# Cross-attention in a decoder layer: twelve stretches of tiles a unit instead of sixteen, whole projections, and the side work of ScalarE, VectorE, GpSimd and the DMA queue at other slots

## The chip, the core and the metric

One core of a Trainium2 chip. The metric is device microseconds of one execution. TensorE (PE) multiplies into eight PSUM banks of 128x512 floats; VectorE (DVE), ScalarE (ACT) and GpSimd (POOL) work beside it; SyncE (SP) issues the DMAs of the stage told of here, all into one queue. Each engine runs its own instructions strictly in order, and engines wait for each other with semaphores.

## What is computed

A post-norm decoder layer on x of 16 batches of 256 rows of 512: self-attention with low-rank corrections, cross-attention over the channel axis, and a gated feed-forward with fp8 rounding, each followed by an addition and a layer norm. The change is in the cross-attention, where x and c are 256x512 per batch (256 channels, 512 positions), with 16 heads of 16 channels:

```python
q = jnp.einsum('oc,bct->bot', Wq, x) + bq[None, :, None]
k = jnp.einsum('oc,bct->bot', Wk, c) + bk[None, :, None]
v = jnp.einsum('oc,bct->bot', Wv, c) + bv[None, :, None]
scores = jnp.einsum('bhkt,bhks->bhts', q, k) * SCALE
p = jax.nn.softmax(scores, axis=-1)
out = jnp.einsum('bhts,bhks->bhkt', p, v)
x = _layernorm(x + Wo @ out + bo)
```

## The kernel before, in words

The program is a list of slots. Each engine has a generator for each phase (self-attention, cross-attention, feed-forward), and a list of turns interleaves the phases: the start of the cross-attention lies beside the end of the self-attention, the end beside the start of the feed-forward, and some 900 of its 1162 slots stand alone.

**Units and tiles.** A unit is half of a batch (8 heads), so there are U = 32 units, and a new one begins every S = 32 slots. An E tile is a 128x512 tile of scores for the exponential, an M tile the same product with the sides swapped, from which the row maximum is taken beforehand. In the steady stage a slot issues one E tile of one unit (L1271) and one M tile of a later unit (L1279); they use opposite halves of the PE rows. ScalarE turns an E tile into probabilities (L1136) and VectorE reduces an M tile to negated maxima (L1314). E tiles rotate over three banks, and so do M tiles: an M tile waits until the reduce of the tile three before it has freed its bank. M tiles of unit u stand in slots 32u+40 to 32u+71, its E tiles from 32u+82.

**Side work of PE.** Each unit has eight groups of values matmuls (L1236, four heads a group, from the probabilities into bank 7) and four projections (q, k, v, and the output projection o; functions `project_part` and `split3`, L85 to L87), all into bank 2. Each projection comes in two parts four slots apart, so 8 + 8 pieces of side work divide a unit's 32 slots into 16 stretches of two slots. A full projection leaves its bank one slot after its last part (`ends_in.get(slot - 1)`), by ScalarE for q, k and v, by VectorE for o, where an addition, BN_STATS and BN_AGGR stand together (L1335 to L1341).

**Stacks.** The float32 scores are made of three products of high and low parts. ScalarE copies the projection out, GpSimd splits it (L1057, L1059), and SP copies it into one of three stacks, six DMAs of 128 KB for q (slot 32u+20) and six for k (32u+25), at L959. The stack of unit u is that of unit u-3, so the q stack waits until the last E tile of u-3 is done (`s_e`), and the first M tile of u waits for all twelve DMAs. In every other unit SP loads the next c (512 KB, L916) between the two.

**Normalising.** Half a unit's output is in bank 7 with its sums. ScalarE copies it to `oc` at slots OUT_AT and OUT_AT + 16 (L1146); SP moves the sums to `xa_sums` one slot on (8 KB, L998); VectorE takes the reciprocal eight slots on (L1345); SP writes them to DRAM (`inv`, 8 KB, L1003) and reads them back, broadcast, into `xa_den` (256 KB, L1011); GpSimd multiplies and adds the halves (L1067, L1072); ScalarE and GpSimd split the sum for the output projection (L1175, L1077). All of these stand in their engines' queues at slots counted from OUT_AT = 101.

Of the kernel before, what the change touches and what calls it, by code (L numbers as in the profile page):

```python
# [15 lines left out]
P = 128  # L16
# [746 lines left out]
XPROBS = 12  # L763
# [3 lines left out]
def cross_attention_phase(nc, ctx, mem, banks, shared, left, a, x1_dram, x2_dram, inv_dram, ones_dram, wg_dram,  # L767
# [30 lines left out]
    prob = values.sb("xa_prob", [P, XPROBS, D], F32)  # L798
# [3 lines left out]
    ol = mem("output").sb("xa_ol", [P, 2, groups, D], F32R)  # L802
# [17 lines left out]
    MAX_AT, TURN_AT, EXP_AT = S + 8, 2 * S + 10, 2 * S + 18  # L820
    BATCH = 2 * S
    OUT_AT = EXP_AT + 19
# [3 lines left out]
    part_slots = {}  # L826
    for u in range(U):
        part_slots["q", u] = [S * u + 2, S * u + 6]
        part_slots["k", u] = [S * u + 10, S * u + 14]
    for b in range(NB):  # L830
        part_slots["v", b, 0] = [BATCH * b + 26, BATCH * b + 30]
        part_slots["v", b, 1] = [BATCH * b + 50, BATCH * b + 54]
        part_slots["o", b, 0] = [BATCH * (b + 2) + 58, BATCH * (b + 2) + 62]
        part_slots["o", b, 1] = [BATCH * (b + 3) + 18, BATCH * (b + 3) + 22]
    for t in range(CC):
        part_slots["o", NB - 1, t] = [BATCH * (NB + 1) + n for n in ((26, 58), (60, 62))[t]]
    slot_of = {j: slots[-1] for j, slots in part_slots.items()}
    at = {j: n for n, j in enumerate(sorted(slot_of, key=lambda j: slot_of[j]))}
    parts_in, ends_in = {}, {}
    for job in part_slots:  # L840
        ends_in.setdefault(slot_of[job], []).append(job)
        for i, slot in enumerate(part_slots[job]):
            parts_in.setdefault(slot, []).append((job, i))
# [7 lines left out]
    def in_turn(count, two, three, begin):  # L851
        at_bank = [two[n % 2] if n < begin else three[n % 3] for n in range(count)]
        before = [max((m for m in range(max(0, n - 4), n) if at_bank[m] == at_bank[n]), default=None)
                  for n in range(count)]
        return at_bank, before

    mb, mb_before = in_turn(len(m_order), (3, 4), (3, 4, 1), (S + 1) * 4)
    eb, eb_before = in_turn(S * U, (5, 6), (5, 6, 0), S * 2)
    SLOTS = range(max(slot_of.values()) + 12)
# [80 lines left out]
    def sync(sp):  # L940
# [38 lines left out]
        for slot in SLOTS:  # L979
# [19 lines left out]
            if (un := output_half(slot, 9)):  # L999
# [5 lines left out]
            if (un := output_half(slot, 14)):  # L1005
# [14 lines left out]
            for job in ends_in.get(slot - 9, []):  # L1020
# [17 lines left out]
    def gpsimd(pool):  # L1038
# [9 lines left out]
        for slot in SLOTS:  # L1048
            yield
            for job in ends_in.get(slot - 2, []):  # L1050
                if job[0] in "qk":
# [28 lines left out]
            if (b := batch(slot, -17)):  # L1080
                low_x(pool, wait, b)
# [713 lines left out]
```

## Times and profile before

| | us |
|---|---|
| median of 3 runs | 2126.02 (2120.32 to 2133.86) |
| the profiled execution, its own time | 2100.74 |
| its span | 2098.9 |
| busy in the span: PE / DVE / ACT / POOL | 1948.0 / 1513.9 / 1133.2 / 997.0 |
| of the 600 us from 1000 to 1600, cross-attention alone: PE / DVE / ACT / POOL | 590.44 / 485.41 / 477.26 / 266.69 |
| one reduce of an M tile (L1314), mean | 0.681 |
| granted PE clock there | 0.99 of full speed |
| share of the 16 DMA engines busy there, and GB/s | 0.63, 112 |

PE is busy for nearly the whole of the steady stage, but a busy PE is not one at its peak: of matmuls that run at once each is counted, and a matmul's end is modelled. All DMAs in the stage are issued by SP.

### The profile page before, as it was taken

The page shows a single profiled execution, that of the slowest core. Times are in us where ns is not written, and L with a number is a line of the kernel's source. Part 1 is how long each engine was busy: PE and PEld are TensorE (multiplying, and loading weights), DVE is VectorE, ACT ScalarE, POOL GpSimd, SP SyncE. Part 2 cuts the span into 40 slices and gives each one's busy share as a digit, 9 for nine tenths or more (in the row PEclk, how much of TensorE's full clock was granted, in tenths as well). Part 3 has the DMA queues.
Part 4 walks back from the last instruction along what each step waited for, and adds up shares of the span by engine and source line. Part 5 has one row for each costly group of instructions (what it writes and reads, how often), then busy time and mean ns, then how long its engine had stood idle before and what let it go on. Part 6 is the DMA issues. An engine that isn't in the chain of part 4 may idle for free.

```text
span 2098.9 us, 31715 instructions
## 1 busy us (share of the span) xinstructions
PE 1948.0 (93%) x11390; PEld 1045.0 (50%) x11424; DVE 1513.9 (72%) x2635; ACT 1133.2 (54%) x2117; POOL 997.0 (47%) x980
## 2 busy tenths in 40 slices
PE   3799999899999888999999999999999898999997
PEld 1667777677767643344434444444444333444443
DVE  4246585566656656777878888887888728999997
ACT  3144444344434433677878877887888673333331
POOL 6345455455554531444444444443444326666664
PEclk9899999999999877999999999999999989999999
DMA  4678786777778653556776655556665510111111
GB/s 138 114 132 138 157 144 130 144 135 161 148 124 150 117 98 52 87 89 127 133 123 112 109 106 107 107 108 103 113 101 105 152 53 11 51 41 41 41 61 41
DMA packets 149515, 220.55 MB, mean 105 GB/s; under 512 B 41463, under 2 KB 50167, under 8 KB 148615
## 3 DMA queue, kind: packets, MB, share of 16 engines
q1 hardware_dynamic: 139886, 217.74, 53.7%
q10 hardware_dynamic: 9472, 0.79, 0.4%
q8 instruction: 90, 1.47, 0.4%
q14 instruction: 67, 0.55, 0.1%
HBM read 83.95 MB, written 32.02 MB: 55 GB/s over the span
## 4 chain that ended last, share of the span: by engine, by line
PE 52%; DMA 19%; DVE 12%; POOL 6%; ACT 3%; issue 3%; SPq 3%; ACTq 0%; POOLq 0%; DVEq 0%
PE bank L1565 7%; PE bank L1236 7%; PE bank L1271 7%; PE bank L85 6%; DMA xa_sums<-xa_oc 5%; PE bank L1541 4%; PE bank L86 4%; PE bank L87 4%; PE bank L1279 4%; DMA sa_kst<-sa_part_kl 4%; DMA inv<-xa_sums 4%; PE bank L506 3%; DMA xa_den<-inv 2%; PE bank L531 2%; DVE sa_mneg L574 2%
## 5 line engine op out<-in xcount | busy, mean ns | idle before, releaser
L1314 DVE TENSOR_REDUCE xa_mneg<-bank 128x1 f32<-128x512 f32 x1024 | 657.8, 681 | 193.7 <-PE bank L1279 190.1
L1136 ACT ACTIVATE xa_prob<-bank 128x512 f32<-128x512 f32 x1024 | 568.9, 600 | 204.9 <-PE bank L1271 195.7
L1279 PE MATMUL bank<-xa_kst,xa_qst 48*128 48x512 f32 x1024 | 411.3, 475 | 23.1 <-DVE xa_mneg L1314 14.9
L1271 PE MATMUL bank<-xa_qst,xa_kst 49*128 49x512 f32 x1024 | 398.4, 460 | 14.3 <-ACT xa_prob L1136 13.9
L402 ACT ACTIVATE sa_prob<-bank 128x512 f32<-128x512 f32 x256 | 152.4, 598 | 370.3 <-PE bank L531 369.7
L1271 PEld LDWEIGHTS bank<-xa_qst,xa_kst 49*128 49x128 f32 x1024 | 161.7, 189 | 329.5 <-ACT xa_prob L1136 257.6
L1236 PE MATMUL bank<-xa_prob,xa_v 128*32 128x512 f32 x2048 | 283.8, 627 | 0.0
L1473 POOL TENSOR_TENSOR ff_total<-ff_prod,ff_mag 128x512 f32<-128x512 bf16 x128 | 194.5, 1520 | 108.6 <-DVE ff_mag L1589 108.6
L574 DVE TENSOR_REDUCE sa_mneg<-bank 128x2 f32<-128x512 f32 x256 | 164.2, 682 | 51.6 <-PE bank L543 51.3
L1279 PEld LDWEIGHTS bank<-xa_kst,xa_qst 48*128 48x128 f32 x1024 | 164.0, 190 | 58.5 <-DVE xa_mneg L1314 38.4
L1517 ACT ACTIVATE ff_gelu<-bank 128x512 bf16<-128x512 f32 x128 | 75.5, 592 | 160.9 <-PE bank L1565 158.7
L1057 POOL CAST xa_part_q<-xa_raw_q 128x512 fp32r<-128x512 f32 x32 | 19.5, 610 | 269.7 <-ACT xa_raw_q L1154 248.0
L531 PE MATMUL bank<-sa_qst,sa_kst 97*128 97x256 f32 x512 | 113.8, 306 | 15.0 <-DMA sa_qst<-sa_mrow 15.0
L531 PEld LDWEIGHTS bank<-sa_qst,sa_kst 97*128 97x128 f32 x512 | 93.5, 196 | 60.1 <-issue 28.6
L1541 PE MATMUL bank<-ff_wo,ff_hq 128*128 128x512 bf16 x504 | 117.2, 385 | 5.3 <-DVE ff_hq L1596 4.6
L1565 PE MATMUL bank<-ff_xq,ff_wg 128*128 128x512 bf16 x498 | 116.5, 383 | 3.4 <-ACT ff_gelu L1517 1.8
L1565 PE MATMUL bank<-ff_xq,wg 128*128 128x512 bf16 x500 | 114.2, 382 | 2.0 <-ACT ff_gelu L1517 1.0
L543 PE MATMUL bank<-sa_kst,sa_qst 96*128 96x256 f32 x512 | 93.9, 301 | 16.6 <-DVE sa_mneg L574 7.9
L1582 DVE TENSOR_TENSOR ff_prod<-bank,ff_gelu 128x512 bf16<-128x512 f32 x128 | 87.1, 680 | 22.6 <-PE bank L1565 18.6
L588 DVE TENSOR_TENSOR sa_xnat<-bank,sa_xnat 128x512 f32<-128x512 f32 x128 | 87.2, 681 | 19.9 <-PE bank L87 18.4
L344 POOL CAST sa_part_qh<-sa_raw 128x512 fp32r<-128x512 f32 x32 | 19.5, 610 | 155.3 <-DMA sa_kst<-sa_part_kl 129.3
L543 PEld LDWEIGHTS bank<-sa_kst,sa_qst 96*128 96x128 f32 x512 | 76.2, 201 | 24.5 <-DVE sa_mneg L574 16.4
(185 smaller groups left out, 3730.6 us busy)
## 6 DMA issues: line engine op xcount, KB each, us to landing
xa_qst<-xa_part_q SPq DMA_DIRECT2D x192, 128.0 KB, 5.4
xa_kst<-xa_part_k SPq DMA_DIRECT2D x192, 128.0 KB, 6.8
sa_qst<-sa_part_qh SPq DMA_DIRECT2D x64, 256.0 KB, 6.2
sa_kst<-sa_part_kh SPq DMA_DIRECT2D x64, 256.0 KB, 9.0
xa_den<-inv SPq DMA_DIRECT2D x64, 256.0 KB
sa_xraw<-xT SPq DMA_DIRECT2D x8, 1024.0 KB, 8.5
sa_qst<-sa_part_ql SPq DMA_DIRECT2D x32, 256.0 KB, 6.0
sa_kst<-sa_part_kl SPq DMA_DIRECT2D x32, 256.0 KB, 10.3
```

The source lines that it names most:

```text
L402: act.activation(prob[:, e % PROBS, :, :], eb[e % 2][:, :], ACT.Exp, scale=S_SCALE)\
L531: last = pe.matmul(eb[e % 2][:, t * L:(t + 1) * L], k[0:97, j, b * L + t * P:b * L + (t + 1) * P], q[0:97, j, b * L:(b + 1) * L], start=Tr ...
L543: last = pe.matmul(mb[m % 2][:, t * L:(t + 1) * L], q[0:96, j, b * L + t * P:b * L + (t + 1) * P], k[0:96, j, b * L:(b + 1) * L], start=Tr ...
L574: dve.tensor_reduce(mneg[:, u % 2, 4 * j + 2 * b:4 * j + 2 * b + 2], mb[m % 2][:, :].rearrange("p (t n) -> p t n", t=2), AX.X, ALU.max, ne ...
L1136: act.activation(prob[:, e % XPROBS, :], banks[eb[e]][:, :], ACT.Exp, scale=X_SCALE)\
L1236: last = pe.matmul(ob[32 * j:32 * j + 32, :], v[(u // 2) % 2][:, t, half, 4 * (u % 2) + j, :], prob[:, (S * u + 4 * quad + j) % XPROBS, :] ...
L1271: pe.matmul(banks[eb[e]][:, :], kst[u % 3][rows_of, head // 2, t * P:(t + 1) * P], qst[u % 3][rows_of, head // 2, :], start=True, stop=Tru ...
L1279: pe.matmul(banks[mb[m]][:, :], qst[u % 3][rows_of, n // 8, t * P:(t + 1) * P], kst[u % 3][rows_of, n // 8, :], start=True, stop=True).the ...
L1314: dve.tensor_reduce(mneg[:, u % 2, column:column + 1], banks[mb[m]][:, :], AX.X, ALU.max, negate=True).then_inc(s_mfree, 1)
L1473: pool.tensor_tensor(total[:, n % 4, :], prod[:, n % 4, :], mag[:, n % 4, :], ALU.add).then_inc(s_hs, 1)
L1541: last = pe.matmul(lb[n % 2][:, :], hq[p % 2][:, h, t * P:(t + 1) * P], wo[:, h, :], start=(h == 0), stop=(h == HT - 1))
L1565: last = pe.matmul(banks[n % 2][:, :], wg[q][:, k, c, h % 4 * P:(h % 4 + 1) * P], xq[p % 2][:, c, :], start=(c == 0), stop=(c == DC - 1))
```

## The change

Projections are issued whole, in one slot, at 2 (q), 10 (k), 18 (o) and 26 (v) of every 32, and values groups in slots of their own that alternate three and five slots apart. So 12 pieces of side work divide a unit, with two or three slots of tiles between them. E tiles start two slots later, the work counted from OUT_AT moves five slots and is drawn closer together, ScalarE, VectorE and GpSimd leave the projection bank three to six slots after the projection, and there are 16 probability tiles, each its own tensor, instead of 12. Buffers of the feed-forward move to make room for four of them; its work is the same. The start of its turns follows the last E tile.

```diff
-XPROBS = 12
+XPROBS = 12, 16
...
-    MAX_AT, TURN_AT, EXP_AT = S + 8, 2 * S + 10, 2 * S + 18
+    MAX_AT, TURN_AT, EXP_AT = S + 8, 2 * S + 10, 2 * S + 20
     BATCH = 2 * S
-    OUT_AT = EXP_AT + 19
+    GROUP = 4
+    VALUES_AT = (EXP_AT + 9, EXP_AT + 12)
+    OUT_AT = EXP_AT + 22
...
-        part_slots["q", u] = [S * u + 2, S * u + 6]
-        part_slots["k", u] = [S * u + 10, S * u + 14]
+    LEAVES = {"q": 3, "k": 6, "v": 3, "o": 3}
+        slot_of["q", u] = S * u + 2
+        slot_of["k", u] = S * u + 10
...
+            slot_of["v", b, t] = BATCH * b + S * t + 26
+            slot_of["o", b, t] = BATCH * (b + 2) + S * t + 50
...
-            if (un := output_half(slot, 9)):
+            if (un := output_half(slot, 7)):
...
-            if (un := output_half(slot, 14)):
+            if (un := output_half(slot, 11)):
...
-            if (un := output_half(slot, 21)):
+            if (un := output_half(slot, 16)):
...
-            if (un := unit(slot, OUT_AT + 41, 1)):
+            if (un := unit(slot, OUT_AT + 35, 1)):
...
-            if (un := unit(slot, EXP_AT + 34, 1)):
-                values(un[0], 7)
-            if (un := unit(slot, EXP_AT + 6, S - 7)) and un[1] % 4 == 0:
-                values(un[0], un[1] // 4)
+            for odd in range(2):
+                if (un := unit(slot, VALUES_AT[odd])) and un[1] % (2 * GROUP) == 0:
+                    values(un[0], un[1] // GROUP + odd)
...
-            for job, i in parts_in.get(slot, []):
-                project_part(job, i)
+            for job in jobs_in.get(slot, []):
+                for i in range(2):
+                    project_part(job, i)
...
-            for job in ends_in.get(slot - 1, []):
+            for job in jobs_in.get(slot - LEAVES["o"], []):
...
-            if (un := output_half(slot, 8)):
+            if (un := output_half(slot, 6)):
                 k = 2 * un[0] + un[1]
                 wait.wait_ge(s_sums, 16 * (k + 1))
                 dve.reciprocal(sums[:, :], sums[:, :]).then_inc(s_inv, 1)
```

Unchanged are the slots of the stacks (STACK_AT = 20 and 25), of the M tiles (MAX_AT), and of the loads of c and x.

SP's queue in one unit of the steady stage, one in which c is loaded too. `xa_qst` and `xa_kst` are the stacks, `xa_sums` and `inv` the sums and their reciprocals, `xa_oc` 134 or 145 is the first half and 135 or 146 the second. Before:

```order
L959 DMA xa_qst_129<-xa_part_q 16x4x512 [waits xa_e,xa_pl]
L959 DMA xa_qst_129<-xa_part_q 16x4x512 x5
L998 DMA xa_sums<-xa_oc_135 128x1x16 [waits xa_oc1]
L916 DMA xa_craw<-c 128x2x512 [waits xa_xlow,xa_xhi]
L959 DMA xa_kst_128<-xa_part_k 16x4x512 [waits xa_pl]
L959 DMA xa_kst_128<-xa_part_k 16x4x512 x5
L1003 DMA inv<-xa_sums 4x32x16 [waits xa_den1,xa_inv]
```

Now:

```order
L965 DMA xa_qst_129<-xa_part_q 16x4x512 [waits xa_e,xa_pl]
L965 DMA xa_qst_129<-xa_part_q 16x4x512 x5
L1017 DMA xa_den_147<-inv 128x1x512 [waits xa_o,xa_back]
L922 DMA xa_craw<-c 128x2x512 [waits xa_xlow,xa_xhi]
L965 DMA xa_kst_128<-xa_part_k 16x4x512 [waits xa_pl]
L965 DMA xa_kst_128<-xa_part_k 16x4x512 x5
L1004 DMA xa_sums<-xa_oc_146 128x1x16 [waits xa_oc1]
L1030 DMA x<-xa_x_0_117 128x512 [waits xa_y]
L1009 DMA inv<-xa_sums 4x32x16 [waits xa_den1,xa_inv]
```

The sums of the second half stood between the two stacks and now stand behind the k stack; the first half's `xa_den` stood ahead of the q stack and now stands behind it.

VectorE's queue over the same slots: TENSOR_REDUCE frees an M tile's bank, `xa_mrow` is the turned row of maxima, SCALAR_TENSOR_TENSOR to BN_AGGR take an output projection out of its bank. Before:

```order
L1345 RECIPROCAL xa_sums<-xa_sums 128x16 [waits xa_sums]
L1314 TENSOR_REDUCE xa_mneg<-bank 128x1 [waits xa_mb] x2
L1335 SCALAR_TENSOR_TENSOR xa_x_1_118<-bank,xa_bo,xa_x_1_118 128x512 [waits xa_pj]
L1338 BN_STATS xa_stats<-xa_x_1_118 128x6 [waits xa_pjfree]
L1341 BN_AGGR xa_mv<-xa_stats 128x2 [waits xa_nm,xa_bn]
L1314 TENSOR_REDUCE xa_mneg<-bank 128x1 [waits xa_mb] x11
L1327 CAST xa_mrow<-bank 32x128 [waits xa_row0,xa_mb]
L1314 TENSOR_REDUCE xa_mneg<-bank 128x1 [waits xa_mb] x3
L1345 RECIPROCAL xa_sums<-xa_sums 128x16 [waits xa_sums]
```

Now:

```order
L1348 SCALAR_TENSOR_TENSOR xa_x_1_118<-bank,xa_bo,xa_x_1_118 128x512 [waits xa_pj]
L1351 BN_STATS xa_stats<-xa_x_1_118 128x6 [waits xa_pjfree]
L1354 BN_AGGR xa_mv<-xa_stats 128x2 [waits xa_nm,xa_bn]
L1327 TENSOR_REDUCE xa_mneg<-bank 128x1 [waits xa_mb] x11
L1358 RECIPROCAL xa_sums<-xa_sums 128x16 [waits xa_sums]
L1327 TENSOR_REDUCE xa_mneg<-bank 128x1 [waits xa_mb] x10
L1340 CAST xa_mrow<-bank 32x128 [waits xa_row0,xa_mb]
L1327 TENSOR_REDUCE xa_mneg<-bank 128x1 [waits xa_mb] x6
L1358 RECIPROCAL xa_sums<-xa_sums 128x16 [waits xa_sums]
```

The reciprocal of the second half stood behind the reduce of slot 29 of 32 and now stands behind that of slot 0, with the reduces of slots 1 to 10 behind it; that of the first half moved from slot 13 to 16.

## Rows read from the trace of the kernel before

**Rows 1.** The rows of L1290 from 1000 to 1600 us, one each unit.
```profile
L1290 PE MATMUL bank<-ident,xa_mneg x21: 283/284/397, 1019.3 to 1573.7; 128*32 128x128 f32 x21
```

**Rows 2.** Timeline of PE: start, us, engine, line, operation, names, count, [idle before].
```profile
1011.18 1.07 PE L1236 MATMUL bank<-xa_prob,xa_v 128*32 128x512 f32 x8
1012.18 0.50 PE L1271 MATMUL bank<-xa_qst,xa_kst 49*128 49x512 f32 x1
...
1012.85 0.50 PE L85 MATMUL bank<-xa_xh,xa_wqh 128*128 128x512 f32 x1
1013.18 0.40 PE L86 MATMUL bank<-xa_xh,xa_wql 128*128 128x512 f32 x1
1013.42 0.39 PE L87 MATMUL bank<-xa_xl,xa_wqh 128*128 128x512 f32 x1
1013.74 0.49 PE L1271 MATMUL bank<-xa_qst,xa_kst 49*128 49x512 f32 x1
```

**Rows 3.** Timeline of SP's queue, two units; us is the issuing, not the transfer.
```profile
1277.51 3.85 SPq L959 DMA_DIRECT2D xa_qst<-xa_part_q  x6
...
1282.58 3.77 SPq L959 DMA_DIRECT2D xa_kst<-xa_part_k  x6
1288.45 0.55 SPq L1003 DMA_DIRECT2D inv<-xa_sums  x1
...
1296.06 0.65 SPq L1011 DMA_DIRECT2D xa_den<-inv  x1
...
1302.04 0.58 SPq L1003 DMA_DIRECT2D inv<-xa_sums  x1
1304.02 0.64 SPq L1011 DMA_DIRECT2D xa_den<-inv  x1
1304.76 4.11 SPq L959 DMA_DIRECT2D xa_qst<-xa_part_q  x6
...
1309.90 3.78 SPq L959 DMA_DIRECT2D xa_kst<-xa_part_k  x6
1316.47 0.55 SPq L1003 DMA_DIRECT2D inv<-xa_sums  x1
1319.49 0.65 SPq L1011 DMA_DIRECT2D xa_den<-inv  x1
```

**Rows 4.** The same of two more units, the slowest of each kind.
```profile
1053.77 3.85 SPq L959 DMA_DIRECT2D xa_qst<-xa_part_q  x6
...
1074.70 0.65 SPq L1011 DMA_DIRECT2D xa_den<-inv  x1
...
1194.13 4.29 SPq L959 DMA_DIRECT2D xa_qst<-xa_part_q  x6
...
1211.27 0.65 SPq L1011 DMA_DIRECT2D xa_den<-inv  x1
```

**Rows 5.** Timeline of PE at a unit's last E tile.
```profile
1303.81 0.49 PE L1271 MATMUL bank<-xa_qst,xa_kst 49*128 49x512 f32 x1
```

**Rows 6.** Timeline of VectorE around a reciprocal and an output projection.
```profile
1316.19 0.25 DVE L1345 RECIPROCAL xa_sums<-xa_sums 128x16 f32<-128x16 f32 x1 [0.67 <-DMA xa_sums<-xa_oc]
...
1317.50 0.74 DVE L1335 SCALAR_TENSOR_TENSOR xa_x<-bank,xa_bo,xa_x 128x512 f32<-128x512 f32 x1
...
1319.10 2.45 DVE L1314 TENSOR_REDUCE xa_mneg<-bank 128x1 f32<-128x512 f32 x4
```

**Rows 7.** Busy time by stretch: PE, PEld, DVE, ACT, POOL, PE clock, DMA, GB/s.
```profile
1071.00:1075.00 4.00, 1.37 (x10) 0.51 (x8) 1.17 (x2) 2.37 (x5) 0.37 (x1) 1.00 0.41 86
1075.00:1078.50 3.50, 3.50 (x15) 1.17 (x15) 1.52 (x3) 0.87 (x2) 1.51 (x2) 0.51 0.51 140
...
1660.00:1673.00 13.00, 8.09 (x29) 3.12 (x26) 5.03 (x9) 4.24 (x9) 3.80 (x3) 0.61 0.14 49
```

**Rows 8.** The chain that ended last, 1200 to 1300 us: start, us, what.
```profile
1241.22 3.80 DMA xa_den<-inv
...
1246.45 1.29 POOL xa_of L1072
```

More of the change, by code:

```diff
@@ L797, in cross_attention_phase @@
     oh = r.sb("xa_oh", [P, 2, groups, D], F32R)
-    prob = values.sb("xa_prob", [P, XPROBS, D], F32)
+    prob = [values.sb(f"xa_prob{n}", [P, D], F32) for n in range(XPROBS[0])]
     oc = [rounding.sb(f"xa_oc{n}", [P, D], F32) for n in range(2)]
@@ L801, in cross_attention_phase @@
     of = parts.sb("xa_of", [P, D], F32)
-    ol = mem("output").sb("xa_ol", [P, 2, groups, D], F32R)
+    output = mem("output")
+    ol = output.sb("xa_ol", [P, 2, groups, D], F32R)
+    prob += [output.sb(f"xa_prob{n}", [P, D], F32) for n in range(*XPROBS)]
     r = mem("cross_small")
@@ L848, in cross_attention_phase, with in_turn @@
     m_at = {job: n for n, (_, _, job) in enumerate(sorted(m_order, key=lambda m: m[:2]))}
-    def in_turn(count, two, three, begin):
-        at_bank = [two[n % 2] if n < begin else three[n % 3] for n in range(count)]
-        before = [max((m for m in range(max(0, n - 4), n) if at_bank[m] == at_bank[n]), default=None)
+    def in_turn(count, few, more, begin):
+        places = [few[n % len(few)] if n < begin else more[n % len(more)] for n in range(count)]
+        before = [max((m for m in range(max(0, n - 2 * len(more)), n) if places[m] == places[n]), default=None)
                   for n in range(count)]
-        return at_bank, before
+        return places, before
     mb, mb_before = in_turn(len(m_order), (3, 4), (3, 4, 1), (S + 1) * 4)
     eb, eb_before = in_turn(S * U, (5, 6), (5, 6, 0), S * 2)
+    place, prob_before = in_turn(
+        S * U, range(XPROBS[0]), [*range(*XPROBS), *range(XPROBS[0])], S * 2)
     SLOTS = range(max(slot_of.values()) + 12)
@@ L1068, in gpsimd @@
                     .then_inc(s_o, 1)
-            if (un := unit(slot, OUT_AT + 39, 1)):
+            if (un := unit(slot, OUT_AT + 34, 1)):
                 u = un[0]
@@ L1133, in scalar @@
                 wait.wait_ge(s_e, e + 1)
-                wait.wait_ge(s_av, (e - XPROBS) // 4 + 1)
-                left.values(wait)
-                act.activation(prob[:, e % XPROBS, :], banks[eb[e]][:, :], ACT.Exp, scale=X_SCALE)\
+                if prob_before[e] is not None:
+                    wait.wait_ge(s_av, prob_before[e] // GROUP + 1)
+                elif place[e] < XPROBS[0]:
+                    left.values(wait)
+                else:
+                    left.output(wait)
+                act.activation(prob[place[e]][:, :], banks[eb[e]][:, :], ACT.Exp, scale=X_SCALE)\
                    .then_inc(s_exp, 1)
@@ L1225, in mb_free, with values @@
                 wait.wait_ge(s_mfree, mb_before[m] + 1)
-        def values(u, quad):
-            half, t = quad // 4, quad % 4
-            wait.wait_ge(s_exp, S * u + 4 * quad + 4)
+        def values(u, group):
+            half, t = group // 4, group % 4
+            wait.wait_ge(s_exp, S * u + GROUP * (group + 1))
             wait.wait_ge(s_pjfree, at["v", u // 2, 1] + 1)
@@ L1742, in build @@
         start += size
-    stretches["output_rest"] = stretches["output"][0] + 8192, 12288
+    stretches["output_rest"] = stretches["output"][0] + 16384, 4096
+    stretches["sums_rest"] = stretches["sums"][0] + 8192, 4096
     def mem(name):
```

64 lines of the change are left out of this document (30 added, 34 removed).

## The prediction, made before the changed kernel was run

> **What bounds the kernel now.** I read the busy time of the steady stage first, then the timeline of PE to price each piece of its program, then the period of a unit, and then SP's queue and the chain, to see what fills the difference. The transpose of L1290 comes once a unit: 20 units in 554.4 us, 27.7 us each [rows 1]. PE's own work is less. From the starts: two slots of tiles 0.67, a group of values 1.00, half a projection 0.89 [rows 2]. A unit has 32 slots, 8 groups and 8 halves: 10.7 + 8.0 + 7.1 = 25.8 us. So 1.9 us of each unit are waits, though PE looks busy. The engines that follow have room (VectorE 485 and ScalarE 477 of 600 us), so the waits are for particular things.
>
> The one that matters is the queue of DMAs. The q stack is issued 0.95 us after the start of the E tile that frees its buffer [rows 5, 3]. Then twelve stack DMAs, the sums, and every other unit c go out. When all of it has landed is seen by a small transfer issued behind it: `inv` is 8 KB, and SP issues `xa_den` as soon as it lands. With nothing ahead that takes 1.98 us (1302.04 to 1304.02); behind a k stack and c 7.6 (1288.45 to 1296.06), behind a k stack alone 3.0 [rows 3]. The small transfer lands with the big ones ahead of it. From the issue of the q stack to that landing it is 18.55 us in the unit with c and 14.7 in the one without [rows 3]; the slowest of each are 20.9 and 17.1 [rows 4]. I take 18.55 and, between 14.7 and 17.1, 15.8.
>
> The Trainium skill (DMA: Bandwidth & Descriptors, Queues, rings and completion order) says that completion in general is not first in, first out per issuing engine, since a DMA spread over few of the 16 engines owes nothing to the others. By that a small transfer might land early; here the rows show it does not.
>
> **The change, part by part.** I count slots modulo 32, with 36 for slot 4 of the next unit.
>
> *PE's own time.* The second half of a whole projection costs three more matmuls, L86 and L87 start 0.24 apart: 0.72 instead of 0.89 [rows 2]. A projection is 1.61 and a unit 10.7 + 8.0 + 6.4 = 25.2 us, 0.7 less. Fewer stretches of tiles save nothing more: a slot of tiles costs 0.335 wherever it stands.
>
> *The output projection on VectorE.* It holds the queue for 1.60 us (1317.50 to 1319.10), and reduces follow 0.6 apart [rows 6]. It now stands behind the reduce of slot 21. Tile 21 issued at 0, that reduce starts at about 1.1, the projection is left at 1.7, the reduces of 22 and 23 start at 3.3 and 3.9 and free their banks about 0.7 later, at 4.0 and 4.6. PE (values at 21 and 24) wants M tiles 25 and 26 at 3.35 and 3.7. It loses 0.9 us, about what such waits cost before.
>
> *ScalarE, probabilities.* Its copies now stand where PE does a values group or a projection; 16 tiles give the later groups room. I price this at nothing: the cover is its 20% of idle time. Without it each would cost its own 0.6 us.
>
> *Sums of the second half.* This is the term that decides. SP had them between the stacks; now they are behind the k stack in order, so they are issued only when those twelve DMAs are out, and land with them. VectorE's reciprocal waits for them behind the reduce of slot 32, and the reduces of 33 to 42 are behind the reciprocal. With three banks, M tiles 33 to 35 still go; M tile 36 needs the reduce of 33. Already before, the reciprocal waited 0.67 us for its sums [rows 6], there behind only the q stack.
> Count from E tile 19, the last of its unit. Sums land at 0.95 + 15.8 = 16.75 us (with c 0.95 + 18.55 = 19.5). The next reduce follows 0.2 after the reciprocal, which is 0.25 long, starts, and the bank is free 0.7 later (a reduce is 681 ns in the mean): M tile 36 starts at 17.65 (20.4). PE comes to it by 17 slots, 4 groups and 2 projections: 5.7 + 4.0 + 3.2 + 0.9 = 13.8. So it stands 3.8 us (6.6).
> From M tile 36 to the next E tile 19 are 15 slots, 4 groups, 2 projections and 0.3 for reduces in a row: 5.0 + 4.0 + 3.2 + 0.3 = 12.5. The period is 30.15 us without c and 32.9 with it.
> This holds wherever a k stack stands just ahead of second-half sums: stacks of units 3 to 31, 29 of them, 13 with c. Mean (16 x 30.15 + 13 x 32.9) / 29 = 31.4, against 27.7: **+3.7 x 29 = +107 us**.
>
> *The clock.* When PE waited 2.6 us for a k stack in 1071 to 1075, the granted clock was 0.51, the lower level of 1.2 GHz, in the following 3.5 us [rows 7]. Half of 3.5 us is lost: 1.7. After each of 29 longer waits: **+49 us**. Bounds: nothing, and 5.1 us a time (148), as in 1660 to 1673, where PE had two waits close together and the mean clock was 0.61, 13 x 0.39 [rows 7]; I take the row with one wait.
> The Trainium skill (TensorE: Matmul & The Clock Gate, HAM oscillation) describes a loop that waits for a DMA at each step and starts every step at the low clock. The trace agrees as far as its one long wait goes. By that rule the lower bound of nothing is unlikely.
>
> *The first M tile.* It waits for the k stack (slot 40). Stacks start two slots later, with the E tiles, but now PE is already late by more, so this adds nothing to the above. If the sums did not stall, it would be next (below).
>
> *The rest of the chain.* After the sums come `inv` (1.98), `xa_den` (3.8), a multiply and an addition, 1.3 each: 8.5 us [rows 3, 8]. The copy of the result at slot 45 comes 6.9 + 0.5 us after M tile 36, itself 0.9 after the sums: 8.3. It is just in time, and adds 0 to 0.3 us a unit. The first half's sums have nothing large ahead of them. The head, the three last units and the feed-forward: two to five slots each, below 5 us, 0.
>
> **Sum.** 2100.7 + 107 + 49 = 2257 us in the profiled execution's own time. The median of the runs shown is 25.3 us above that execution, so 2282 in their terms.
>
> **The rivals.**
> 1. *The sums stall, the clock stays up*: +107, 2233. For it: with 1.9 us of waits in each unit the stage's clock was 0.99. Against: those are in several pieces, and the one piece of 2.6 us did bring it down.
> 2. *The sums do not stall* (they land early, as the skill's sentence allows, or VectorE has them in time). Then the k stack sets the time at M tile 40: 0.95 + 18.4, then 11 slots, 3 groups and 2 projections, 9.9: 29.25 with c, and 0.95 + 15.6 + 9.9 = 26.45 without (18.4 and 15.6 are the landings above less 0.2 for the small transfer); mean 27.7, as before: 2126, no change. It decides if a small transfer behind six big ones takes below 3 us; rows 3 speak against it.
> 3. *Faster*: neither stall; the stage runs at PE's 25.2 + 0.9 = 26.1 us, -1.6 x 29 = -46: 2080. It needs the stacks with c to land within about 16 us of their issue, against 18.55.
> 4. *Worse*: the clock falls for longer after the waits of 6.6 us and the copy at slot 45 comes late too: 2282 + 96 = 2378.
>
> **Chances.** Forecast with the clock loss 0.58, rival 1 0.20, rival 4 0.06: slower 0.84. Rival 2 0.09, rival 3 0.07. Some of rival 2's place lies beyond 1% to either side, but evenly. A difference of 1%, 21 us, is about what can be told from no change. The range reaches from rival 1 with the shortest landings of rows 3 (14.7 for 15.8, 16 x 1.1 = 18 us less, and as much again on the units with c: 2195) to the forecast with the clock loss at 4 us a time (2350); it leaves the forecast's neighbours 2 and 3 out.
>
> **What would show it.** Right: the reciprocal behind slot 32 waits 4 to 8 us for `xa_sums`; M tile 36 has the largest idle time of PE, released by VectorE; the period of L1302, the transpose, is near 30 and 33 us in turn plus the clock's part; PE's granted clock falls once a unit; landing of `xa_sums` has two clusters, about 2 us and 6 to 9. Wrong: periods near 27 with waits at M tile 40 for `xa_kst` (rival 2), or a period of 26 (rival 3). What would make it wrong is a sums transfer that overtakes the k stack, or k stacks that start earlier than the last E tile allows.

## The result, and the profile after

The changed kernel takes 2332.7 us (median of 4 runs, 2323.5 to 2339.8), the kernel before, run beside it, 2123.2 (2102.9 to 2133.9): a ratio of 1.100 with a 95% interval of 1.091 to 1.109. It is slower by 10%. The profiled execution's own time is 2323.5 us with a span of 2321.7, so 223 us more than the 2100.7 of before, where the prediction has 156.

The steady stage shows the whole of it. Its row of busy time, from 1000 to 1600 us (columns: stretch, us, busy PE, PEld, DVE, ACT, POOL, then PE clock, share of the DMA engines, GB/s):

```profile
1000.00:1600.00 600.00, 480.15 (x2659) 216.63 (x2659) 365.97 (x636) 359.44 (x686) 210.17 (x217) 0.88 0.54 87
```

Every engine has a fifth to a quarter less work in it than before, the DMA engines too (112 GB/s before), and the granted clock fell from 0.99 to 0.88. No engine became the bound; waits did. The transpose that comes once a unit is L1302 now:

```profile
L1302 PE MATMUL bank<-ident,xa_mneg x17: 283/284/286, 1016.6 to 1589.2; 128*32 128x128 f32 x17
```

That is 572.6 us for 16 units, 35.8 each, against 27.7 [rows 1]. The 8.1 us more, over the 29 units that the prediction counts, would be 235, so the stage holds the whole loss. Waits of the same stretch (who, for whom: us in all, times, the longest):

```profile
DVE xa_sums L1358 <- DMA xa_sums<-xa_oc: 143.1, 17, 10.0
PEld bank L1292 <- DVE xa_mneg L1327: 135.5, 49, 8.7
POOL xa_of L1075 <- DMA xa_den<-inv: 123.5, 17, 8.5
PE bank L1292 <- DVE xa_mneg L1327: 118.2, 33, 8.3
```

One wait a unit, 8.4 us in the mean, for the second half's sums; and PE's wait for the reduce queued behind it. From the page of the whole execution, the line of the chain that ended last (shares of the span), and the group of the reciprocal (count | busy, mean ns | idle before it, and for what):

```profile
PE 41%; DMA 20%; SPq 11%; DVE 11%; ACT 7%; POOL 5%; issue 3%; ACTq 0%; POOLq 0%; DVEq 0%
...
L1358 DVE RECIPROCAL xa_sums<-xa_sums 128x16 f32<-128x16 f32 x64 | 15.9, 248 | 253.7 <-DMA xa_sums<-xa_oc 253.7
```

One unit with c, followed through three timelines (start, us, engine, line, what, [idle before]). SP's queue:

```profile
1311.18 3.81 SPq L965 DMA_DIRECT2D xa_qst<-xa_part_q  x6
1315.10 0.66 SPq L1017 DMA_DIRECT2D xa_den<-inv  x1
1315.86 0.40 SPq L922 DMA_DIRECT2D xa_craw<-c  x1
1316.31 5.16 SPq L965 DMA_DIRECT2D xa_kst<-xa_part_k  x6
1321.52 0.59 SPq L1004 DMA_DIRECT2D xa_sums<-xa_oc  x1
```

VectorE:

```profile
1319.73 2.58 DVE L1327 TENSOR_REDUCE xa_mneg<-bank 128x1 f32<-128x512 f32 x4
1331.00 0.25 DVE L1358 RECIPROCAL xa_sums<-xa_sums 128x16 f32<-128x16 f32 x1 [8.69 <-DMA xa_sums<-xa_oc]
1331.17 3.01 DVE L1327 TENSOR_REDUCE xa_mneg<-bank 128x1 f32<-128x512 f32 x5
```

PE, where the matmul that waits is M tile 36:

```profile
1319.86 0.50 PE L1284 MATMUL bank<-xa_qst,xa_kst 49*128 49x512 f32 x1
...
1320.90 1.06 PE L1249 MATMUL bank<-xa_prob,xa_v 128*32 128x512 f32 x8
...
1324.15 0.50 PE L1292 MATMUL bank<-xa_kst,xa_qst 48*128 48x512 f32 x1
1324.49 0.39 PE L1284 MATMUL bank<-xa_qst,xa_kst 49*128 49x512 f32 x1
1331.85 1.39 PE L1292 MATMUL bank<-xa_kst,xa_qst 48*128 48x512 f32 x2 [6.98 <-DVE xa_mneg L1327]
1332.45 0.62 PE L1284 MATMUL bank<-xa_qst,xa_kst 49*128 49x512 f32 x1
1333.17 1.94 PE L1249 MATMUL bank<-xa_prob,xa_v 128*32 128x512 f32 x8
```

The sums are issued at 1321.52, as soon as SP is through with the k stack, and are there at 1331.0, 19.8 us after the q stack's issue. The reduces, 0.6 apart till 1322.3, stop. PE has three banks, uses them, and stands for 7 us. Then it goes on at about half speed: the values group of L1249 takes 1.94 us where the one before the wait took 1.06. The granted clock by stretch, columns as above:

```profile
1312.00:1323.00 11.00, 10.74 (x72) 5.14 (x65) 9.34 (x16) 8.72 (x19) 1.35 (x5) 1.00 1.00 149
1323.00:1333.00 10.00, 3.02 (x12) 1.74 (x10) 2.00 (x5) 1.60 (x4) 1.14 (x1) 0.78 0.67 102
1333.00:1340.00 7.00, 7.00 (x32) 2.31 (x31) 3.87 (x7) 3.58 (x7) 4.43 (x4) 0.58 0.34 112
```

### The profile page after: what moved, and what is told of

Same layout as the page of the kernel before. It is cut to its first block, busy times and chain, and to the rows that moved or that the text cites. A ratio compares the mean times of both kernels' runs of the same rounds, so it can differ in the third digit from the quotient of the medians.

```text
span 2321.7 us, 31753 instructions
## 1 busy us (share of the span) xinstructions
PE 1982.9 (85%) x11424; PEld 1090.1 (47%) x11424; DVE 1497.9 (65%) x2635; ACT 1118.1 (48%) x2117; POOL 1000.8 (43%) x980
## 4 chain that ended last, share of the span: by engine, by line
PE 41%; DMA 20%; SPq 11%; DVE 11%; ACT 7%; POOL 5%; issue 3%; ACTq 0%; POOLq 0%; DVEq 0%
DMA xa_sums<-xa_oc 13%; SPq L965 9%; PE bank L1578 6%; PE bank L1249 5%; PE bank L1284 5%; PE bank L85 5%; ACT xa_prob L1148 4%; DMA sa_kst<-sa_part_kl 4%; PE bank L87 4%; PE bank L86 4%; PE bank L1554 4%; PE bank L1292 3%; PE bank L506 3%; PE bank L531 2%; DVE xa_mneg L1327 1%
## 5 line engine op out<-in xcount | busy, mean ns | idle before, releaser
L1327 DVE TENSOR_REDUCE xa_mneg<-bank 128x1 f32<-128x512 f32 x1024 | 642.6, 682 | 218.9 <-PE bank L1292 217.8
L1148 ACT ACTIVATE xa_prob<-bank 128x512 f32<-128x512 f32 x1024 | 550.5, 608 | 403.8 <-PE bank L1284 400.1
L1292 PE MATMUL bank<-xa_kst,xa_qst 48*128 48x512 f32 x1024 | 426.7, 508 | 201.9 <-DVE xa_mneg L1327 199.4
L1284 PE MATMUL bank<-xa_qst,xa_kst 49*128 49x512 f32 x1024 | 389.8, 470 | 16.2 <-ACT xa_prob L1148 16.1
L1284 PEld LDWEIGHTS bank<-xa_qst,xa_kst 49*128 49x128 f32 x1024 | 181.0, 203 | 328.7 <-ACT xa_prob L1148 221.8
L1249 PE MATMUL bank<-xa_prob,xa_v 128*32 128x512 f32 x2048 | 312.4, 686 | 0.0
L1292 PEld LDWEIGHTS bank<-xa_kst,xa_qst 48*128 48x128 f32 x1024 | 185.0, 207 | 259.9 <-DVE xa_mneg L1327 240.3
L1358 DVE RECIPROCAL xa_sums<-xa_sums 128x16 f32<-128x16 f32 x64 | 15.9, 248 | 253.7 <-DMA xa_sums<-xa_oc 253.7
L1075 POOL TENSOR_TENSOR xa_of<-xa_oc,xa_den 128x512 f32<-128x512 f32 x32 | 40.9, 1279 | 216.1 <-DMA xa_den<-inv 216.1
L1595 DVE TENSOR_TENSOR ff_prod<-bank,ff_gelu 128x512 bf16<-128x512 f32 x128 | 87.2, 681 | 17.9 <-ACT ff_gelu L1530 12.3
```

What stands on the lines that cost most here:

```text
L1148: act.activation(prob[place[e]][:, :], banks[eb[e]][:, :], ACT.Exp, scale=X_SCALE)\
L1249: last = pe.matmul(ob[32 * j:32 * j + 32, :], v[(u // 2) % 2][:, t, half, 4 * (u % 2) + j, :], prob[place[S * u + GROUP * group + j]][:, : ...
L1284: pe.matmul(banks[eb[e]][:, :], kst[u % 3][rows_of, head // 2, t * P:(t + 1) * P], qst[u % 3][rows_of, head // 2, :], start=True, stop=Tru ...
L1292: pe.matmul(banks[mb[m]][:, :], qst[u % 3][rows_of, n // 8, t * P:(t + 1) * P], kst[u % 3][rows_of, n // 8, :], start=True, stop=True).the ...
L1327: dve.tensor_reduce(mneg[:, u % 2, column:column + 1], banks[mb[m]][:, :], AX.X, ALU.max, negate=True).then_inc(s_mfree, 1)
```

## The experiments

Times are medians, each with its ratio to the kernel before on the same chip. The median of the kernel before was 2102 to 2105 us beside the variants in the table and 2123 beside the changed kernel, so where a text below takes one time from another and the ratios say less, both are given. A period is worked out as above, from the first and last transposes between 1000 and 1600 us.

| kernel | us | ratio (95%) | period |
|---|---|---|---|
| changed | 2332.7 | 1.100 (1.091 to 1.109) | 35.8 |
| sums_act | 2324.7 | 1.105 (1.095 to 1.114) | 35.2 |
| store_late | 2338.2 | 1.112 (1.101 to 1.123) | 35.8 |
| before_sums_behind | 2279.1 | 1.083 (1.069 to 1.097) | 34.8 |
| recip_late | 2276.4 | 1.082 (1.069 to 1.094) | 33.7 |
| den_first | 2238.5 | 1.065 (1.059 to 1.072) | 32.5 |
| k_after_sums | 2194.9 | 1.043 (1.031 to 1.055) | 30.9 |
| k_sums_c_y | 2183.2 | 1.038 (1.030 to 1.046) | 30.6 |
| k_sums_c | 2141.5 | 1.018 (1.008 to 1.028) | 28.9 |
| k_sums_c_den | 2137.7 | 1.017 (1.012 to 1.021) | 28.4 |
| k_split | 2127.4 | 1.011 (1.004 to 1.017) | 28.2 |
| before_c_late | 2092.5 | 0.994 (0.990 to 0.998) | 28.1 |

Where a text below says when a transfer landed, that is from the trace's records of its completion, as a mean over the units from 1000 to 1600 us, counted from the issue of that unit's q stack. In the changed kernel the second half's sums land at 18.4 us in units without c and 20.6 in units with c, 0.1 to 0.2 us behind the last piece of the k stack.

The theory was that of the prediction: the second half's sums stand behind the k stack, and that alone is most of the loss. Its rivals were that the loss lies in something else of the change, and, for the reason why small transfers land late, SP's queue against the DMA engines.

### The sums' place, put into the old kernel

```diff
--- before
-            if (un := output_half(slot, 1)):
+            if (un := output_half(slot, 1)) and un[1] == 0 or (un := output_half(slot, 5)) and un[1] == 1:
                 u, half = un
                 ...
                 sp.dma_start(sums[:, :], sum_rows).then_inc(s_sums, 16)
```

> The kernel before, with one thing of the change alone: the second half's sums are issued behind the k stack (four slots later in SP's queue), the reciprocal stays at its place. Theory: the loss is reproduced without whole projections or twelve stretches. Sums land 16 to 18 us after the q stack's issue, M tile 33 then waits, period 30.5 to 33 us plus the clock's part against 27.7, time 2240 to 2340. Rival (the loss is from stretches of three tiles, bank rotation or later exponentials): 2126 within 20 us.

Measured: 2279 us. One 8 KB transfer a unit, issued four slots later in an otherwise unchanged kernel, costs 8.3%. Waits of its stage:

```profile
DVE xa_sums L1345 <- DMA xa_sums<-xa_oc: 100.4, 18, 9.3
...
PE bank L1279 <- DVE xa_mneg L1314: 71.4, 18, 7.7
```

and its row of busy time has the clock at 0.87, from 0.99. Here the sums land at 14.5 us without c and 17.6 with it, and the M tile that waits is 33, because the reciprocal stands behind reduce 29 and not 32: from M tile 32 to 33 it is 4.3 and 7.2 us, for 1.3 before. What follows: the place of the sums suffices for most of the loss, without anything else of the change. How much of the 10% it makes up is not given by this run, since the reciprocal stands three reduces earlier and `xa_den` elsewhere than in the changed kernel.

### The k stack behind the sums

```diff
--- changed
-            if (un := unit(slot, STACK_AT + 5, 1)):
+            if (un := unit(slot, STACK_AT + 8, 1)):
                 stack("k", un[0])
```

> The changed kernel with the k stack moved behind the second half's sums and the store of x in SP's queue (slot 28 instead of 25), all else equal. Theory: sums no longer behind the k stack, the reciprocal waits below 2 us, but SP waits for ScalarE's copy first, so the k stack lands some 3 us later and the M tile of slot 40 waits: period near 32 us, time about 2230. Rival (SP's own time for issuing is what costs): the sum of issues is unchanged and so is the time, 2330.

Measured: 2195 us, 138 less than the changed kernel (by the ratios, 1.100 and 1.043, 120). The wait for the sums is down from 143 to 36 us, and M tile 40 waits for the k stack instead:

```profile
DVE xa_sums L1358 <- DMA xa_sums<-xa_oc: 35.9, 10, 4.6
PEld bank L1292 <- DMA xa_kst<-xa_part_k: 25.1, 17, 2.0
```

What is left of the sums' wait falls in units with c, whose 512 KB stand ahead of them. Undoing the one order gives back 120 to 138 of the 210 us.

### The queue or the engines

```diff
--- changed
+            if (un := output_half(slot, 1)) and un[1] == 1:
+                ...
+                act.dma_start(sums[:, :], sum_rows).then_inc(s_sums, 16)
```

> The changed kernel, but the sums of the second half are issued by ScalarE, on its own DMA queue, one slot after the copy that they need, instead of by SP behind the k stack. Theory (the reciprocal waits because the sums stand behind twelve stack DMAs in one queue): the sums land within 4 us, VectorE's wait before the reciprocal falls from about 8.5 us a unit to below 1, PE's largest wait moves from the M tile of slot 36 to that of slot 40 (k stack), the period falls from 35.8 to about 30 us, the time to about 2160 us. Rival (the 16 DMA engines are simply full, whichever queue issues): sums still land 6 us or more after their issue, time 2290 or more.

Measured: 2325 us; my theory was wrong in this point. ScalarE's queue issues the sums while SP is in the middle of the k stack, and they land at 18.2 and 20.2 us, 0.2 to 0.4 sooner. Timelines of ScalarE's queue, SP's and VectorE, in that order:

```profile
1107.45 0.55 ACTq L1155 DMA_DIRECT2D xa_sums<-xa_oc  x1
```
```profile
1100.09 3.83 SPq L965 DMA_DIRECT2D xa_qst<-xa_part_q  x6
1104.02 0.66 SPq L1017 DMA_DIRECT2D xa_den<-inv  x1
1104.78 0.39 SPq L922 DMA_DIRECT2D xa_craw<-c  x1
1105.23 3.82 SPq L965 DMA_DIRECT2D xa_kst<-xa_part_k  x6
```
```profile
1121.61 0.25 DVE L1364 RECIPROCAL xa_sums<-xa_sums 128x16 f32<-128x16 f32 x1 [10.40 <-DMA xa_sums<-xa_oc]
```

Issued at 1107.45, there at 1121.6: 14.2 us for 8 KB, where the first half's sums, as large and with nothing large ahead, take 1.9 in every unit. So what holds the small transfer is not its place in the issuing queue but what is in flight on the engines behind both queues. It need not have been issued first: two pieces of the k stack and the store of x were issued on SP's queue after 1107.45, and the records have them landing at 1119.5, 1121.1 and 1121.4, all ahead of the sums. The Trainium skill (DMA: Bandwidth & Descriptors, Queues, rings and completion order) says that a DMA's semaphore increment lands only after every earlier write of that DMA engine, across its queues. The trace agrees as far as it goes: the sums landed after all four pieces of the k stack that were issued before them, the last at 1117.6. What the prediction took from the same section, that a small DMA may land early, no run here showed.

### What stands just behind

```diff
--- changed
-            for job in jobs_in.get(slot - 9, []):
+            for job in jobs_in.get(slot - 9, []) + jobs_in.get(slot - 16, []):
```
(with a condition that keeps the last two batches at 9)

> The changed kernel with the store of x (256 KB) that follows the second half's sums in SP's queue moved seven slots on, behind the reciprocals' write; the sums still stand behind the k stack. Theory (a transfer lands only when the DMA engines have drained what is in flight, also what was issued just behind it): stack and sums land 1.3 to 2 us sooner, period 34 to 34.5 us against 35.9, time 2280 to 2295. Rival (only what stands ahead counts): 2325 within 10.

Measured: 2338 us, period 35.8. The 256 KB store issued right behind the sums adds nothing to them: they land at 18.6 and 20.6 us. This is shown for one store on the same queue; sums_act above, and k_split below, have transfers that were issued after the sums and landed ahead of them.

### The reciprocal behind reduce 36

```diff
--- changed
-            if (un := output_half(slot, 6)):
+            if (un := output_half(slot, 6)) and un[1] == 0 or (un := output_half(slot, 10)) and un[1] == 1:
                 ...
                 dve.reciprocal(sums[:, :], sums[:, :]).then_inc(s_inv, 1)
```

> The changed kernel with VectorE's reciprocal of the second half four slots later, behind the reduce of slot 36; the sums land as late as before. Theory (VectorE's order turns a late landing into a PE stall): PE passes the M tiles of slots 36 to 39 before the wait, which moves to slot 40, 2.6 us a unit are won there, and 1.7 are given back at ScalarE's copy of the result (slot 45), which waits for the chain from the reciprocal on: about 28 us less, 2305. Rival (the landing alone sets the period, whatever stands behind the reciprocal): same time within 10 us.

Measured: 2276 us, 56 less (by the ratios 38), and so more than the 28 expected; the period is 2.1 us shorter, and little of the 1.7 us that was to be given back at slot 45 shows.

```profile
PE bank L1292 <- DVE xa_mneg L1327: 89.3, 36, 6.3
DVE xa_sums L1358 <- DMA xa_sums<-xa_oc: 85.7, 18, 6.3
```

PE comes to the stall four tiles later, and the stall is that much shorter (85.7 / 18 = 4.8 for 8.4), but it is the same one: the landing stays, at 18.4 and 20.5 us.

### The DMA that the prediction had not counted

At this point the landing itself was unexplained: some 2 us later than [rows 3]. The change moves `xa_den` of the first half from slot 19 to slot 21, and the q stack stays at 20. So 256 KB that were issued ahead of both stacks ([rows 3]: 1304.02, then the q stack at 1304.76) now stand between them (1315.10 above).

```diff
--- changed
-            if (un := output_half(slot, 11)):
+            if (un := output_half(slot, 9)) and un[1] == 0 or (un := output_half(slot, 11)) and un[1] == 1:
                 ...
                 sp.dma_start(den[half][:, :], spread).then_inc(s_den[half], 16)
```

> The changed kernel, with one DMA moved: SP issues the first half's `xa_den` (256 KB, a broadcast read of eight rows) at slot 19, ahead of the q stack, where the kernel before had it, and not at slot 21 between the q and the k stack. Theory: this DMA between the stacks is what made their landing later than in the trace of before (q stack's issue to the last piece of the k stack: 18.0 to 18.3 us in units without c and 20.0 to 20.9 with c, against 15.2 and 18.4). Moved ahead, the landing is back at 15.5 to 16.5 and 18.5 to 19; the reciprocal's wait for xa_sums falls from 8.4 us each to about 6.3; the period from 35.8 to 33.5 us; 29 units by 2.2 us is 64 less: 2255 to 2280 us. Rival: the bytes in flight are the same and only their order changes, so the landing, the wait (8.4) and the time (2320 to 2340) stay.

Measured: 2238.5 us, 94 less than the changed kernel (by the ratios, 1.100 and 1.065, 73), and more than I had expected. The sums land at 14.8 us without c and 17.9 with it, 3.6 and 2.7 sooner. The rows of the transpose, and of the waits:

```profile
L1302 PE MATMUL bank<-ident,xa_mneg x19: 283/284/286, 1004.8 to 1588.9; 128*32 128x128 f32 x19
```
```profile
DVE xa_sums L1358 <- DMA xa_sums<-xa_oc: 100.7, 18, 8.8
```

From the last E tile to M tile 36 it is now 16.6 us without c and 19.7 with it, for 19.9 and 22.0 in the changed kernel (means over the units from 1000 to 1600, from the starts of the two matmuls); the prediction has 17.65 and 20.4. Its landings of 15.8 and 18.55 were right within 1 us for the order of before, and the change had moved one more DMA than it counted. Units without c gain twice: the stall (from M tile 35 to 36 it is now 3.1 us for 6.4) also costs less clock, so that the way from M tile 36 to the next unit's E tile 19 falls from 14.7 to 13.7 us.

That mean hides steps. The 6 us behind M tile 36 in three units, where it had started 2.0, 2.9 and 5.9 us after M tile 35 (columns as above; the clock is the third number from the end):

```profile
1196.00:1202.00 6.00, 6.00 (x36) 2.59 (x36) 5.56 (x10) 4.33 (x8) 3.09 (x3) 1.00 0.13 45
1583.00:1589.00 6.00, 6.00 (x31) 1.85 (x31) 4.21 (x8) 3.03 (x6) 3.15 (x3) 0.72 0.14 45
1228.00:1234.00 6.00, 6.00 (x27) 2.08 (x29) 3.99 (x7) 2.75 (x5) 2.54 (x3) 0.59 0.39 132
```

In the two units where M tile 36 came 2.0 and 2.2 us after 35, the rest of the way takes 12.5 and 12.6 us, as PE's own time has it; in the seven with 2.3 to 4.4 us it takes 14.0 each, and in the ten with 4.7 to 7.9 us 14.6 to 15.4.

### Towards a faster version

Three kernels, each built on the one before it and all on k_after_sums, take first the load of c and then the first half's `xa_den` out of the way, and then split the k stack.

```diff
--- k_after_sums
-            if (b := batch(slot, -40)):
+            if (b := batch(slot, -22)):
                 load_c(sp, wait, b)
```

> The kernel with the k stack behind the sums, and also the load of c 18 slots later, outside the stretch from the q stack to the M tile of slot 40. Theory (what lies in flight between the two stacks sets the period): the units with c lose their extra 3.5 us, the period is 28.5 to 29.5 in all units against 28.5 and 33 in turn, time 2130 to 2160. Rival (DMA volume over the whole unit counts, not its place): 2195 within 15.

Measured: 2141 us, period 28.9. The alternation of long and short units is gone, the sums' wait too. Of PE's waits for a DMA these are left, 1.7 us at M tile 40 where an undisturbed tile has 0.3 (the largest wait in the list, 137.1 us of weight loads for the probabilities, was 172.0 in the kernel before):

```profile
PEld bank L1292 <- DMA xa_kst<-xa_part_k: 31.8, 21, 2.3
PE bank L1292 <- DMA xa_kst<-xa_part_k: 21.7, 20, 1.8
```

```diff
--- k_sums_c, as den_first
+            if (un := output_half(slot, 9)) and un[1] == 0 or (un := output_half(slot, 11)) and un[1] == 1:
```

> The kernel k_sums_c (k stack behind the second half's sums, c loaded 18 slots later) with the first half's `xa_den` ahead of the q stack too. Theory: M tile 40 still waits for the k stack there (3.0 us at slot 40, the stack landing 16.6 to 17.1 us after the q stack's issue, of which 8.5 us go by before it is issued at all). With the den gone from between, the q stack has drained when the k stack starts, so that it lands 0.5 to 1 us earlier: period 28.9 to 28.2, 2115 to 2140 us. Rival: the k stack's time counts from its own issue, behind the sums, and the den between is through by then anyway: period 28.9, 2141 us.

Measured: 2138 us, period 28.4. The time lies in the theory's range and 0.2% from the rival's, so it does not decide; the landings do, for the rival: the k stack is issued 8.5 us after the q stack and lands at 16.8 us in both kernels. What a moved DMA is worth depends on what waits behind it.

```diff
--- k_sums_c_den
+            if (un := unit(slot, STACK_AT + 5, 1)):
+                stack("k", un[0], (0, 3))
-                stack("k", un[0])
+            if (un := unit(slot, STACK_AT + 8, 1)):
+                stack("k", un[0], (3, 6))
```

> As k_sums_c_den, but the k stack is split: its first three DMAs stand right behind the q stack, the second half's sums behind them, and its last three behind the sums. Theory: when the sums are issued, 7.5 us after the q stack's issue, there are three and not six pieces of the k stack in flight ahead of them, so they land within 4 us, before M tile 36 can be wanted (13.8 us after E tile 19); and the last three pieces land at about 14 us, before M tile 40 comes. Neither wait is left: period 26 to 27.5 us, 2050 to 2095 us, faster than the kernel before. Rival: with PE earlier, the next transfer in line (the chain den, multiply, add, copy at slot 45, or the projection at slot 18 that waits for ScalarE's copy of the k projection) takes the place of the waits: period 27.5 to 28.5, 2095 to 2130 us. Second rival: nine pieces in flight hold the sums up as twelve do: period 30 or more, above 2180 us.

Measured: 2127 us, 1.1% slower than before; inside the first rival's range. The k stack has left the list of waits, but the sums are held up again. They land at 13.2 us, 6.1 after their issue and not within 4:

```profile
DVE xa_sums L1362 <- DMA xa_sums<-xa_oc: 49.9, 21, 3.7
PEld bank L1296 <- DVE xa_mneg L1331: 49.2, 80, 2.4
```

In one unit the sums were issued at 1233.8 and landed at 1241.2: the last of the three pieces ahead of them had landed at 1238.9, and two of the three pieces issued behind them at 1240.0 and 1240.7. So half a stack ahead and the other half right behind hold them up together; which of the two weighs more no run separates. (The pieces of a stack count on one semaphore, so a single piece's landing is read from that count.)

The two other attempts missed. k_sums_c_y is k_sums_c with ScalarE's last step of the output projection four slots later (and the store seven):

```diff
--- k_sums_c
-            for job in jobs_in.get(slot - 6, []):
+            for job in jobs_in.get(slot - 10, []):
                 if job[0] == "o":
                     ...
                     act.activation(x, x, ACT.Identity, bias=rstd[:, 2, one], scale=rstd[:, 1, one])
```

> As the one before, and ScalarE's layer-norm scaling of x, which waits for GpSimd ahead of the copy that the sums need, is four slots later, and the store of x behind it moves too. Theory: SP no longer waits about 3 us for the copy between the stacks, the k stack lands 14.5 to 15.5 us after the q stack is issued, PE is the bound, period 26 to 27 us, time 2060 to 2095, below both kernels. Rival (the stall only moves to the next link): 2130 or more.

Measured: 2183 us, 42 more than k_sums_c. ScalarE brings the second half's result sooner, and so SP's queue closes up:

```profile
1200.54 0.66 SPq L1017 DMA_DIRECT2D xa_den<-inv  x1
1202.62 0.59 SPq L1004 DMA_DIRECT2D xa_sums<-xa_oc  x1
1203.26 3.81 SPq L965 DMA_DIRECT2D xa_kst<-xa_part_k  x6
```

The sums are 2.1 us behind the den here; in k_sums_c, whose rows show it at another unit, 3.5:

```profile
1213.45 0.66 SPq L1017 DMA_DIRECT2D xa_den<-inv  x1
1216.90 0.59 SPq L1004 DMA_DIRECT2D xa_sums<-xa_oc  x1
```

and the reciprocal waits for its sums again, 38.0 us in 20 times. By the landings, the sums stand behind the den in both kernels (they land 0.1 us after it in k_sums_c, 0.4 here), and the den takes 8.7 us from its issue, for 6.0 in k_sums_c. Here the k stack follows it by 2.7 us instead of 4.6 (in the units shown) and lands at 18.3 us for 16.8, although it was issued sooner. That the closer spacing is the cause is argued from these rows; no run isolates it, and the store was moved too.

k_split_dve is k_split with the reciprocal behind reduce 34 and the projection's copy on VectorE behind reduce 23:

```diff
--- k_split
-            for job in jobs_in.get(slot - LEAVES["o"], []):
+            for job in jobs_in.get(slot - 5, []) + jobs_in.get(slot - 3, []):
...
-            if (un := output_half(slot, 6)):
+            if (un := output_half(slot, 6)) and un[1] == 0 or (un := output_half(slot, 8)) and un[1] == 1:
```

> The kernel k_split (period 28.24 us) with two moves in VectorE's queue. (1) The second half's reciprocal stands behind the reduce of slot 34, not 32: in k_split the sums land about 12.7 us after the q stack's issue, and PE still loses 1.5 us at slots 36 and 37 to it. (2) The output projection's copy stands behind the reduce of slot 23, not 21: there it costs 1.15 us at slots 25 and 26; behind 23 it has the values group of slot 24 and the projection of slot 26 as cover, and costs 0.5 us there, because the projection waits for its bank. Theory: both waits are local to VectorE's order, so they go and nothing of the same size takes their place: 28.24 - 1.5 - 0.6 = 26.1 us a unit, 31 x 2.1 = 65 us less than k_split: 2050 to 2080 us, 1.5 to 2.5% faster than the kernel before. Rival: with PE earlier at slot 38, the last three pieces of the k stack (14.9 us after the q stack's issue) or the result's copy at slot 45 come late by as much as was gained: period 27.5 to 28.3, 2100 to 2130 us.

One run took 2117 us and five 2149 to 2155, so no verdict is drawn; even the lowest is level with the kernel before beside it (2117), and not 1.5% faster. From the profiled execution, one of 2149 us, I take only what waits: the sums' wait is down from 49.9 us to 5.8, and ScalarE's wait in its last step of the output projection is longer (61.5 us for 35.8 in k_split, up to 2.9 us a time for 1.6), with the probabilities queued behind it and PE behind them (timeline of ScalarE, then waits from 1200 to 1400 us):

```profile
1214.78 0.81 ACT L1197 ACTIVATE xa_x<-xa_x,xa_rstd 128x512 f32<-128x512 f32 x1 [2.93 <-POOL xa_rstd L1110]
```
```profile
PE bank L1288 <- ACT xa_prob L1152: 11.0, 7, 1.6
```

VectorE's part was moved two slots back and ScalarE's, which needs it, was not; that this is what cost the time is not shown. So neither of my two prices can be read from this run.

### The load of c in the kernel before

```diff
--- before
-            if (b := batch(slot, -40)):
+            if (b := batch(slot, -22)):
                 load_c(sp, wait, b)
```

> The kernel before with the load of c alone 18 slots later. Theory: its units with c, 28.5 us against 26.6 without, come down to the others, 13 or 14 times 1.5 to 2 us: 2080 to 2100 against 2105 to 2125. Rival (c's transfer only collides with something else): no change.

Measured: 2092.5 us in 10 runs, ratio 0.994 (0.990 to 0.998). The waits for the k stack that the kernel before had at M tile 40 are gone from the list, and the one for the sums is longer (9.1 us before):

```profile
DVE xa_sums L1345 <- DMA xa_sums<-xa_oc: 21.5, 21, 2.6
```

It is the only kernel here that is below the one before, by 0.6%, which is hardly worth more than a mention. Where the 0.6% comes from is not shown: the period from 1000 to 1600 us is 28.1 us, no shorter than the 27.7 of before, with units of 26.5 to 33.5 us. No version with whole projections was faster than the kernel before.

## Why the prediction was right, and where its terms were off

**The deciding term was right in mechanism.** The sums issued behind the k stack, the reciprocal in VectorE's order behind reduce 32, M tile 36 as the one that waits, two lengths of unit in turn (34.6 us without c and 37.0 with it, for 31.85 and 34.6 in the sum with its clock term): all of it is in the trace, and before_sums_behind and k_after_sums show that this order is most of the cause. Two clusters of landing came too: by the trace's records of the transfers, 1.9 us from issue for the first half's sums and 9 to 12 for the second's, above the 6 to 9 that was named.

**Its size was too small, because one moved DMA was missed.** "I take 18.55 and, between 14.7 and 17.1, 15.8" carries landings of the old order over to the new one. Measured from E tile 19 to M tile 36: 19.9 and 22.0 us, for 17.65 and 20.4; in the mean over the 29 units 2.0 each, 57 us in all. (The landing from the q stack's issue was 2.6 and 2.0 us later than taken; the q stack followed its E tile by 0.6 us instead of 0.95.) den_first shows the cause: the first half's `xa_den`, which the diff moves past the q stack. The working names SP's rows for this DMA as a marker of landings, and never as a transfer in the way.

**The clock term was right in kind and too small.** From M tile 36 to the next E tile 19 the prediction has 12.5 us and 1.7 for the clock, 14.2. Measured 14.7 without c and 14.9 with it: 2.3 for the clock, by the same 12.5, so 17 us more over 29 units. The one wait of 2.6 us in [rows 7] is a poor measure for these, where M tile 36 starts 6.4 and 8.5 us after M tile 35. den_first bears out both numbers: 12.5 us where the clock stayed up, and 1.5 us more in the units with M tile 36 2.3 to 4.4 us after 35, near the 1.7 of [rows 7]; after longer waits 2.1 to 2.9 more.

Together they are 57 + 17 = 74 us, against the 67 by which the profiled execution is beyond the sum. The 7 us between them are not accounted for; the means are from 17 of the 29 units.

**PE's own time was right.** From 1319.86 to 1324.15 above PE does five slots of tiles, a values group and a projection; by the prices of the prediction 5 x 0.335 + 1.00 + 1.61 = 4.29, and measured 4.29.

**The output projection on VectorE**: predicted 0.9 us at M tiles 25 and 26, and in the changed kernel the ways from E tile 25 to 26 and 26 to 27 are 1.10 and 2.31 us in the mean, where an undisturbed slot has 0.34 and one with a projection 1.92: 1.15. Right in place, small in effect.

**M tile 40 and the chain's end** were priced at nothing and stayed hidden, as long as the sums were late; k_after_sums and k_sums_c, where the sums are in time, have the wait for `xa_kst` next, at M tile 40, where rival 2 has it. Rival 2 gave 27.7 us a unit for that with the k stack in its old place; k_sums_c, where it is issued 8.5 us after the q stack and c is out of the way, has 28.9.

**The range**, 2195 to 2350, holds 2332.7; and that is in part luck: the upper end came from a clock loss of 4 us a time, while in fact three quarters of the excess was the landing, for which the range had left no room upwards. The 96 us of rival 4 are not worked out there; 5.1 less 1.7 us in 29 units would be 99.

## What to carry to other kernels

For each DMA that a change moves, write out the new order of issue with bytes, also of those that do not seem to matter, and count for every small transfer on a critical wait all the bytes ahead of it on any queue. Another queue did not help here. What was issued behind made no difference in one case (store_late), but in sums_act and k_split the sums landed after transfers that were issued after them, so large transfers right behind are not free either. A reciprocal of 0.25 us that waits in the order of a busy engine makes the whole engine wait; the price is the landing less the cover of free banks, plus the clock lost after it. When such a stall is removed the next one in line keeps a part of it (one reorder gave back 120 to 138 of 210 us, three more edits 67), so cost the second wait as well.

## What the runs showed of the hardware that I had not expected

- An 8 KB transfer issued on ScalarE's queue, when SP had issued about 2 MB since the start of the q stack, took 14.2 us (11.5 in the median over units); the first half's, with nothing large ahead, 1.9. Two issuing queues were worth 0.6 us in the period.
- 256 KB moved from ahead of two stacks to between them cost 94 us in 29 units, 3.2 us each (73 us and 2.5 by the ratios), close to what the transfer takes with little beside it (3.8 us [rows 8]). The DMA engines were busy for 0.54 of the stage, but for all of the time from 1312 to 1323 us, when the stacks were being issued (share 1.00).
- The clock's loss after a wait came in steps. In den_first it was nothing in the two units where M tile 36 came 2.0 and 2.2 us after 35 (granted clock 1.00 in the 6 us behind), 1.5 us in each of the seven with 2.3 to 4.4 us, and 2.1 to 2.9 in those with more.
